# The next chunk's preparation moved from VectorE to TensorE, ScalarE and GpSimd, and D*u summed in y's bank

## The reference, cut to what matters

```python
up = y @ W_up + b_up                       # y: the normalised rows, normalised again, gamma, beta
left, right = split(up)                    # 128 channels each
u = silu(causal_conv3(left) + conv_b)
delta = softplus(u @ W_delta + b_delta);  Bm = u @ W_B;  Cm = u @ W_C     # 64 states
h = exp(delta * A) * h + (delta * u) * Bm  # token after token, 128 channels x 64 states
y = sum over states of h * Cm  + u * D
s = xn + (y * silu(right)) @ W_down + b_down
g = silu(sum of two experts of (silu(xn @ w1) * (xn @ w3)) @ w2)
out = x + s * g
```

## Time and profile before

| | |
|---|---|
| median of 3 runs | 1525.58 us (1524.34 to 1527.27) |
| profiled execution: its time, its span | 1526.07 us, 1524.3 us |
| busy: TensorE, VectorE, GpSimd, ScalarE | 80%, 80%, 76%, 47% of the span |
| first scan, and the chunks after the first begin | 103.5; 272.6, 437.0, 606.3, 778.3, 941.9, 1109.3, 1282.5 us |

### The profile page before, as it was taken

The page is one execution under the profiler, slowest core; times in us unless marked ns, Lnnn a source line. Parts: engine busy times, 40 slices in busy tenths (PEclk is TensorE's granted clock), DMA queues, the critical chain, the costliest instruction groups (busy, mean ns, idle before and its releaser), DMA issues. The chain is left out here.

```text
span 1524.3 us, 21337 instructions
## 1 busy us (share of the span) xinstructions
PE 1222.2 (80%) x5496; PEld 860.7 (56%) x5496; DVE 1222.3 (80%) x1597; ACT 721.6 (47%) x1557; POOL 1154.3 (76%) x1088
## 2 busy tenths in 40 slices
PE   5737655889988999889989999889988999896720
PEld 5613111566756677556666677657756676674410
DVE  6545999888787978799888987898778988787738
ACT  1445533464544555354555555455535555455611
POOL 0233788779896888778987888789977788799953
PEclk9969655899999999999999999999999999997555
DMA  9843697556564557446655855646744684754336
GB/s 239 168 128 94 169 283 206 150 151 189 172 224 132 171 165 254 129 133 204 220 158 160 250 171 158 228 126 208 232 140 127 181 259 149 255 166 145 121 117 221
DMA packets 173124, 272.52 MB, mean 179 GB/s; under 512 B 28544, under 2 KB 70144, under 8 KB 172992
## 3 DMA queue, kind: packets, MB, share of 16 engines
q10 hardware_dynamic: 111072, 173.93, 39.3%
q1 hardware_dynamic: 55104, 78.41, 16.7%
q0 software_dynamic: 6816, 18.69, 3.2%
HBM read 225.20 MB, written 45.76 MB: 178 GB/s over the span
## 5 line engine op out<-in xcount | busy, mean ns | idle before, releaser
L420 POOL TENSOR_TENSOR arena<-arena,c_rep 128x512 f32<-128x512 f32 x498 | 595.5, 1202 | 183.9 <-DVE arena L924 177.8
L924 DVE TENSOR_TENSOR_SCAN arena<-bank,carry,arena 128x512 f32<-128x512 f32 x512 | 651.9, 1274 | 75.2 <-ACT bank L660 69.9
L1154 PE MATMUL bank<-xgT,wring 128*128 128x256 f32 x2240 | 534.1, 381 | 17.8 <-DVE xn L952 7.1
L660 ACT ACTIVATE bank<-arena,a_neg 128x512 f32<-128x512 f32 x512 | 354.7, 693 | 261.5 <-DVE arena L924 111.0
L1154 PEld LDWEIGHTS bank<-xgT,wring 128*128 128x128 f32 x2240 | 424.0, 190 | 87.7 <-DVE gt L936 13.8
L1123 PE MATMUL bank<-wring,hid 128*128 128x256 f32 x1120 | 301.3, 392 | 44.9 <-ACT o_sb L604 44.6
L914 DVE TENSOR_TENSOR arena<-bank,b_rep 128x512 f32<-128x512 f32 x400 | 272.3, 681 | 40.4 <-PE bank L1166 32.4
L1166 PE MATMUL bank<-stack,pick 128*128 128x512 f32 x400 | 234.7, 598 | 73.3 <-DVE arena L914 51.9
L595 ACT ACTIVATE th<-bank 128x256 f32<-128x256 f32 x312 | 118.9, 381 | 367.6 <-PE bank L1154 309.2
L1123 PEld LDWEIGHTS bank<-wring,hid 128*128 128x128 f32 x1120 | 205.8, 192 | 150.2 <-issue 101.9
L442 POOL TENSOR_TENSOR hid<-gt,ue 128x256 f32<-128x256 f32 x312 | 244.9, 786 | 38.3 <-DVE gt L936 34.9
(11 more groups left out here) (148 smaller groups left out, 744.9 us busy)
## 6 DMA issues: line engine op xcount, KB each, us to landing
arena<-delta_d ACTq DMA_DIRECT2D x512, 256.0 KB, 4.0
arena<-du_d ACTq DMA_DIRECT2D x112, 256.0 KB, 4.2
wring<-in_w_all SPq DMA_DIRECT2D x64, 384.0 KB, 5.5
x_sorted<-arena SPq DMA_DIRECT2D x2, 5031.0 KB, 38.5
xg<-x_sorted ACTq DMA_DIRECT2D x39, 256.0 KB
arena<-results SPq DMA_DIRECT2D x16, 512.0 KB, 6.3
xn<-in_x SPq DMA_DIRECT2D x4, 1024.0 KB, 9.5
parts_d<-spare SPq DMA_DIRECT2D x16, 256.0 KB, 4.2
```

Source lines behind the costliest of these rows:

```text
L420: pool.tensor_tensor(p_ring[:, s % P_RING, :], h_ring[:, s % H_RING, :], of_chunk(c_rep, c, 2), ALU.mult).then_inc(s_hc, 1)
L660: act.activation(a_bank[s % 2][:, :], dl_ring[:, s % D_RING, :], ACT.Exp, scale=a_neg[:, s % PAIRS:s % PAIRS + 1]).then_inc(s_exp, 1)
L924: v.tensor_tensor_scan(out=h_ring[:, s % H_RING, :], data0=a_bank[s % 2][:, :], data1=product_with_b(s), initial=carry[:, q:q + 1], op0=AL ...
L1154: ins = pe.matmul(bank[:, m * SLOT:(m + 1) * SLOT], wring[:, kk, (2 * m + h) * P:(2 * m + h + 1) * P], xgT[:, i % 2, h, :], start=(h == 0) ...
```

## The change

VectorE's fourteen preparation instructions for a chunk and the final add of `gate_chunk` go.

- The convolution becomes three matmuls with diagonal weights (`taps`), a turn of its own at `at` 14; ScalarE evicts it.
- "1 + tanh", the clip, and the "1 + e, less 1" of the log's correction become ScalarE instructions, and so does the rounding of the high part. ScalarE has seven instructions more for a chunk.
- The products and sums of two tensors become seven GpSimd instructions for a chunk: `silu` and `right` at 17 and 18, `sum` in four parts at 25 to 28, `low` at 31.
- D*u is one more matmul with a diagonal weight, the first of a chunk into `y_bank`. SyncE's two stores and the load of `tails` go.
- The turns `delta`, `b` and `c` stand at 20, 23 and 26.

```diff
-WORK_AT = dict(conv=11, tanh=15, silu=16, clip=19, log=20, split=23, store=32, stack=36)
-WORK_PARTS = dict(conv=3, silu=3, log=2, split=7)
-PRODUCT_AT = {18: "delta", 21: "b", 24: "c"}
+WORK_AT = dict(tanh=15, sigmoid=16, silu=17, right=18, exp=22, ln=23, less=24, sum=25, round=30, low=31, store=33, stack=37)
+WORK_PARTS = dict(sum=4)
+PRODUCT_AT = {14: "conv", 20: "delta", 23: "b", 26: "c"}
 DOWN_AT = {6: 0, 8: 1}
-BIAS_AT, TAILS_AT = 61, 16
+BIAS_AT = 61
...
-            return spare[:, dict(cv=0, dlt=0, thl=1, ud=1, thr=2, sr=2, u=3, hi=3, ex=4, ln=5, lo=5, wm=6, du=6)[name], :]
+            return spare[:, dict(thl=0, hi=0, thr=1, du=1, u=2, cv=3, ex=3, ln=4, lo=4, dlt=5, wm=6)[name], :]
...
-        KD = 7
-        STORES = 16 * 6
+        KD, KS_P = 5, 6
+        STORES = 16 * 4
...
-                sp.dma_start(tails_d[:, 0, cols(c)], stage("sr")).then_inc(s_partd, 16)
-                sp.dma_start(tails_d[:, 1, cols(c)], stage("ud")).then_inc(s_partd, 16)
...
-                if at == TAILS_AT:
-                    sp.wait_ge(s_lr, NC)
-                    ge(sp, s_dn, 2 * c)
-                    sp.dma_start(tails[:, :, :], tails_d[:, :, cols(c)]).then_inc(s_tails, 16)
...
+            def silu_of_left(c):
+                pool.wait_ge(s_sig, c + 1)
+                if c:
+                    pool.wait_ge(s_red, QUADS * (c - 1) + 1)
+                pool.tensor_tensor(stage("u"), stage("thl"), stage("cv"), ALU.mult).then_inc(s_u, 1)
+            def gate_of_right(c):
+                pool.wait_ge(s_sig, c + 1)
+                ge(pool, s_dn, 2 * (c - 1))
+                pool.tensor_tensor(sr[:, c % 2, :], stage("thr"), b_rep[:, cols(c)], ALU.mult).then_inc(s_sr, 1)
+            def delta_sum(c, part):
+                base = KD * c
+                if part == 0:
+                    pool.wait_ge(s_sp, KS_P * c + 5)
+                    pool.tensor_tensor(stage("dlt"), stage("dlt"), stage("ln"), ALU.add).then_inc(s_dlt, 1)
+                elif part == 1:
+                    pool.wait_ge(s_sp, KS_P * c + 6)
+                    pool.tensor_tensor(stage("wm"), stage("wm"), stage("ex"), ALU.subtract).then_inc(s_dlt, 1)
+                elif part == 2:
+                    pool.wait_ge(s_dlt, base + 2)
+                    pool.tensor_tensor(stage("dlt"), stage("dlt"), stage("wm"), ALU.subtract).then_inc(s_dlt, 1)
+                else:
+                    pool.wait_ge(s_dlt, base + 3)
+                    pool.wait_ge(s_u, c + 1)
+                    pool.tensor_tensor(stage("du"), stage("dlt"), stage("u"), ALU.mult).then_inc(s_dlt, 1)
+            def low_part(c):
+                pool.wait_ge(s_hi, c + 1)
+                pool.tensor_tensor(stage("lo").bitcast(F32R), stage("du"), stage("hi"), ALU.subtract).then_inc(s_dlt, 1)
+            silu_of_left(0)
+            gate_of_right(0)
+            for part in range(4):
+                delta_sum(0, part)
...
+                for name, c, r in work_at(s):
+                    if name == "silu":
+                        silu_of_left(c)
+                    elif name == "right":
+                        gate_of_right(c)
+                    elif name == "sum":
+                        delta_sum(c, r)
+                    elif name == "low":
+                        low_part(c)
...
+            def evict_conv(c):
+                act.wait_ge(s_cv, c + 1)
+                ge(act, s_partd, STORES * c)
+                act.activation(stage("cv"), product_bank(c, "conv")[:, :], ACT.Identity, bias=half[:, 3:4]).then_inc(s_cvs, 1)
             def tanhs(c):
-                act.wait_ge(s_cv, c + 1)
+                act.wait_ge(s_cvs, c + 1)
                 act.activation(stage("thl"), stage("cv"), ACT.Tanh)
                 act.activation(stage("thr"), b_rep[:, cols(c)], ACT.Tanh).then_inc(s_tanh, 1)
+            def sigmoids(c):
+                act.wait_ge(s_tanh, c + 1)
+                act.activation(stage("thl"), stage("thl"), ACT.Identity, bias=1.0)
+                act.activation(stage("thr"), stage("thr"), ACT.Identity, bias=1.0).then_inc(s_sig, 1)
             def softplus(c, part):
                 if part == 0:
                     act.wait_ge(s_dp, c + 1)
                     act.activation(stage("ex"), product_bank(c, "delta")[:, :], ACT.Abs, bias=vec[:, 10:11]).then_inc(s_sp, 1)
+                    act.activation(stage("dlt"), product_bank(c, "delta")[:, :], ACT.Relu, bias=vec[:, 10:11]).then_inc(s_sp, 1)
                 elif part == 1:
-                    act.wait_ge(s_sp, 3 * c + 1)
+                    act.wait_ge(s_sp, KS_P * c + 1)
                     act.activation(stage("ex"), stage("ex"), ACT.Exp, scale=-1.0).then_inc(s_sp, 1)
+                elif part == 2:
+                    act.wait_ge(s_sp, KS_P * c + 3)
+                    act.activation(stage("wm"), stage("ex"), ACT.Identity, bias=1.0).then_inc(s_sp, 1)
+                    act.activation(stage("ln"), stage("ex"), ACT.Ln, bias=1.0).then_inc(s_sp, 1)
                 else:
-                    act.wait_ge(s_sp, 3 * c + 2)
-                    act.activation(stage("ln"), stage("ex"), ACT.Ln, bias=1.0).then_inc(s_sp, 1)
+                    act.wait_ge(s_sp, KS_P * c + 4)
+                    act.activation(stage("wm"), stage("wm"), ACT.Identity, bias=-1.0).then_inc(s_sp, 1)
+            def high_part(c):
+                act.wait_ge(s_dlt, KD * c + 4)
+                act.activation(stage("hi").bitcast(F32R), stage("du"), ACT.Copy).then_inc(s_hi, 1)
...
+            evict_conv(0)
             tanhs(0)
+            sigmoids(0)
...
-            for c in range(4, NC):
+            softplus(0, 3)
+            scale_rows(4)
+            scale_rows(5)
+            high_part(0)
+            for c in range(6, NC):
...
+            v.wait_ge(s_setup, 1)
+            for tap in range(3):
+                v.tensor_scalar(taps[:, tap, :], ident[:, :], half[:, tap:tap + 1], None, ALU.mult)
+            v.tensor_scalar(taps[:, 3, :], ident[:, :], vec[:, 11:12], None, ALU.mult)
...
-            def conv(c, tap):
-                cv = stage("cv")
-                if tap == 0:
-                    ge(v, s_partd, STORES * c)
-                    v.wait_ge(s_lrev, c + 1)
-                    v.tensor_scalar(cv, of_chunk(c_rep, c, 2), half[:, 2:3], half[:, 3:4], ALU.mult, ALU.add).then_inc(s_cvs, 1)
-                else:
-                    v.wait_ge(s_cvs, 2 * c + tap)
-                    v.scalar_tensor_tensor(out=cv, in0=of_chunk(c_rep, c, 2 - tap), scalar=half[:, 2 - tap:3 - tap],
-                                           in1=cv, op0=ALU.mult, op1=ALU.add).then_inc(s_cvs if tap == 1 else s_cv, 1)
...
-            def silu(c, part):
-                if part == 0:
-                    v.wait_ge(s_tanh, c + 1)
-                    v.scalar_tensor_tensor(out=stage("u"), in0=stage("thl"), scalar=1.0, in1=stage("cv"),
-                                           op0=ALU.add, op1=ALU.mult).then_inc(s_u, 1)
-                elif part == 1:
-                    v.scalar_tensor_tensor(out=stage("sr"), in0=stage("thr"), scalar=1.0, in1=b_rep[:, cols(c)],
-                                           op0=ALU.add, op1=ALU.mult).then_inc(s_ud, 1)
-                else:
-                    v.wait_ge(s_u, c + 1)
-                    v.wait_ge(s_ud, 2 * c + 1)
-                    v.scalar_tensor_tensor(out=stage("ud"), in0=stage("u"), scalar=vec[:, 11:12], in1=stage("sr"),
-                                           op0=ALU.mult, op1=ALU.mult).then_inc(s_ud, 1)
...
-            def clip(c):
-                v.wait_ge(s_sp, 3 * c + 1)
-                v.tensor_scalar(stage("dlt"), product_bank(c, "delta")[:, :], vec[:, 10:11], 0.0, ALU.add, ALU.max
-                                ).then_inc(s_dlt, 1)
...
-            def split(c, part):
-                dlt, du, wm = stage("dlt"), stage("du"), stage("wm")
-                hi, lo = (stage(name).bitcast(F32R) for name in ("hi", "lo"))
-                base = c * KD
-                if part == 0:
-                    v.wait_ge(s_sp, 3 * c + 3)
-                    v.tensor_scalar(wm, stage("ex"), 1.0, -1.0, ALU.add, ALU.add).then_inc(s_dlt, 1)
-                elif part == 1:
-                    v.wait_ge(s_dlt, base + 1)
-                    v.tensor_tensor(dlt, stage("ln"), dlt, ALU.add)
-                elif part == 2:
-                    v.wait_ge(s_dlt, base + 2)
-                    v.tensor_tensor(wm, wm, stage("ex"), ALU.subtract).then_inc(s_dlt, 1)
-                elif part == 3:
-                    v.wait_ge(s_dlt, base + 3)
-                    v.tensor_tensor(dlt, dlt, wm, ALU.subtract).then_inc(s_dlt, 1)
-                elif part == 4:
-                    v.wait_ge(s_dlt, base + 4)
-                    v.tensor_tensor(du, dlt, stage("u"), ALU.mult).then_inc(s_dlt, 1)
-                elif part == 5:
-                    v.wait_ge(s_dlt, base + 5)
-                    v.wait_ge(s_bc, 2 * c + 2)
-                    v.tensor_copy(hi, du).then_inc(s_dlt, 1)
```

(35 more changed lines are left out.)

42 lines of the change are left out of this document (20 added, 22 removed).

## The result

| | before | after |
|---|---|---|
| median (20 runs each) | 1527.03 us (1521.55 to 1530.24) | 1534.34 us (1528.03 to 1539.12) |
| ratio, 95% interval | | 1.0052 [1.0041, 1.0063] |
| profiled execution, its span | 1526.07, 1524.3 us | 1539.12, 1537.3 us |
| first scan | 103.5 us | 107.6 us |
| first chunk | 169.0 us | 173.7 us |

The changed kernel is 0.5% slower, where I forecast 0.7% faster. In the table, a chunk is taken from its first scan to the next chunk's. The parts of the table add up to the 13.0 us between the spans (4.1 + 4.7 + 6.0 - 1.8).

A forecast was written before the change was run, and what follows sets the result against it. TensorE was taken to set the pace at 32 to 63, GpSimd close behind, with VectorE the bound in the first chunk. 1526.1 - 9.6 (six chunks) - 4 (first chunk) + 3 (ahead of the loop) = 1515.5, forecast 1515; range 1495 to 1539.

The forecast's parts named there:

- SyncE's two stores and a load are off the path.: SyncE's queue: the two stores and the load were taken to cost the path nothing.
- (a): Chunk's end: VectorE's final add L945 goes, taking 10 us off TensorE's waits in six chunks; bounds 0 and 17.0.
- (b): Chunk boundaries: with about 2 us less to wait, TensorE's clock stays up, 12 us gained; bounds 0 and 14.
- (c): Gates, clip and B products behind VectorE's preparation: 13 of 16.8 us of TensorE's waits go; bounds 0 and 16.8.
- the convolution: TensorE at 8 to 15, 92% busy: three added products of 0.85 us a chunk hide nowhere, 15.3 us in six chunks.
- My sign: If right: TensorE's busy time at 8 to 15 rises about 2.5 us a chunk and the stretch is no shorter.
- GpSimd's lag: GpSimd, overfull at 24 to 31, falls one pair behind and catches up at 32 to 63: 5 us in six chunks.
- Two signs of "wrong": If wrong: waits for L476 or L411 to L426 over 10 us in all, or a clock below 1 at 24 to 40.
- GpSimd becomes the bound: Rival: preparation overloads GpSimd, hidden products come late, TensorE pauses and its clock drops: 1538 us; chance 0.24.
- The first chunk: First chunk, VectorE the bound: 4 us gained at 16 to 31, where GpSimd may lag; bounds 0 and -5.9.
- Ahead of the loop: Before the first scan: 13.4 us instead of 11.1 from u's first product to the first store; in all +3, bounds -1 and +7.

The follow-up runs named there:

- late_store: The changed kernel with SyncE's four stores at place 40 instead of 33 and the stack load at 48 instead of 37: 1517.89 us, ratio 0.9954.
- early_store: The kernel before with only SyncE's stores and stack load moved, to 27 and 31 instead of 32 and 36: 1558.24 us, ratio 1.0205.
- du_only: The kernel before with D*u alone as a matmul into y's bank, nothing else of the change: 1505.74 us, ratio 0.9874.
- ls_conv: late_store with the convolution back on VectorE at 11 to 13: 1506.46 us, ratio 0.9875.
- ls_both: late_store with the convolution and, in the loop, GpSimd's seven two-input instructions on VectorE: 1505.57 us, ratio 0.9873.
- ls_sums: late_store with GpSimd's seven two-input instructions on VectorE in the loop, at the same places: 1514.06 us, ratio 0.9927.
- mix_three: ls_conv with the second chunk's seven two-input instructions on VectorE; for other chunks, second and third sum and low part there, four on GpSimd: 1499.23 us, ratio 0.9812.
- late_all: The changed kernel with rounding at 34, low part at 36, SyncE's stores at 42 and stack load at 50: 1521.31 us, ratio 0.9982.

## Why the prediction was wrong

**"SyncE's two stores and a load are off the path."** This step failed. It was right for the stores that go, and I took it for the whole queue, so the sum put SyncE at nothing. That SyncE waits for GpSimd's low part, and that the tile's release stands behind it in the same list, was in the kernel (`store` at 33, `load_weights`), and nowhere in my sum. I had followed `high_part` into ScalarE's list, but not `low` into SyncE's. The runs show its price from both sides: 16 us taken away (late_store), 32 us put into the kernel before (early_store). With late_store's 1517.9 us, my 1515 would have been 3 us off, but partly by luck: against before, late_store's 8 to 31 are 7.6 us shorter, where my terms for them (-13, +15.3, +5) make 7.3 longer, and its first chunk is 4.6 us longer, where I had 4 shorter.

**(a) and (b), the boundary.** Right. Forecast -22, plus 5.1 for D*u's matmul (six of 0.85): -17. du_only's 0 to 7 shows -16.4, the changed kernel -14.2. The waits for the gate fell from 17.0 to 6.9 us, and du_only's boundary has the full clock; in the kernel after it is 1.00 in five of the six windows of 0 to 7 and 0.93 in one.

**(c), waits behind VectorE's preparation, and the convolution.** Forecast -13 and +15.3; measured together -9.8 at 8 to 23, and +1.6 at 24 to 31. The convolution alone costs 11.4 us (ls_conv against late_store), so the rest gave about 20, above the 16.8 that I had as (c)'s bound. Of these, du_only has 5.1 at 8 to 23 with the preparation still on VectorE; what of the others was paid back at 32 to 39 is not told apart. My sign, TensorE's busy time at 8 to 15 up by 2.5 us a chunk and the stretch no shorter, did not come: it fell from 141.2 to 138.5 us in all and the stretch by 5.8, with three steps moved out of it. The Trainium skill (SBUF — State Buffer, "Who interferes with whom") had me expect that the instructions moved to GpSimd would meet only VectorE instructions with one input in PSUM. They took 1.27 us instead of the 1.20 of `state_by_c`, and each of the 56 between 1.25 and 1.31, so none was held up. Where the rule does bite, it is as the two pairs of rows of ls_both above have it.

**GpSimd's lag, "5 us; bounds 0 and 15".** As a term it was not too small: in the profiled executions ls_sums has the six chunks 5.1 us and the first chunk 3.5 us shorter than late_store, and the medians differ by only 3.8 in all. What I didn't see is that it also decides when SyncE gets on. I had written that the rival needed a lag of more than two steps; in the timeline above `low` is 5.3 us behind its input, two pairs, and TensorE feels it through SyncE rather than through hidden products (5.5 us, three waits). Two signs of "wrong" came: the clock below 1 at 32 to 39, and ScalarE's waits for L421, 13.3 us over the span. The rival "GpSimd becomes the bound" gave 1538, near the 1534.3 measured, and named the clock's fall (its sum doesn't come out: 15 + 10 on 1515 make 1540, less the 5 already in it 1535); but GpSimd was no bound. It was busy 118.7 of 130.2 us (91%) at 24 to 31, where I had forecast over 95%, and moving SyncE's work alone won the time back.

As to the Trainium skill's rule that speaks against the change (GPSIMD Engine Reference, "Engine selection": two-input elementwise work belongs on VectorE, since GpSimd takes about twice as long): the rows above have 1.27 us on GpSimd against means of 0.72 to 1.50 on VectorE beside it, 1.08 over all seven, so not twice; twice holds against the 0.66 that VectorE takes undisturbed. My 1.84 and 1.90 for VectorE were the two slowest groups of the kernel before, which has 1.16, 1.12 and 1.01 for three of the others (L798, L792, L795). Its advice held where GpSimd was short of time, in the first chunk, and not in the others, where mix_three with four of the seven on GpSimd is the fastest.

**The first chunk, forecast -4, measured +4.7.** Wrong. I had GpSimd at 38.6 us for 16 to 31 and let it lag. The windows of the kernel after for 16 to 31 and 32 to 63:

```profile
170.10:210.50 40.40, 22.01 (x54) 6.42 (x54) 35.15 (x38) 19.11 (x32) 35.31 (x34) 0.61 0.58 147
210.50:281.30 70.80, 41.20 (x105) 12.94 (x106) 66.39 (x71) 23.62 (x41) 62.11 (x57) 0.50 0.85 251
```

One of VectorE's groups at 32 to 63, in the list of groups of that window:

```profile
L970 DVE TENSOR_TENSOR arena<-arena,c_rep 128x512 f32<-128x512 f32 x6 | 6.6, 1094 | 0.0
```

And two rows of the timeline:

```profile
207.13 0.63 ACT L611 ACTIVATE spare<-spare 128x512 fp32r<-128x512 f32 x1 [6.88 <-POOL spare L421]
...
208.48 1.28 DVE L936 TENSOR_TENSOR_SCAN arena<-bank,carry,arena 128x512 f32<-128x512 f32 x1 [3.58 <-ACT bank L733]
```

At 16 to 31 VectorE is idle 5.3 of 40.4 us instead of 1.2 of 39.6: ScalarE's rounding waited 6.88 us for GpSimd's last sum, and the scan 3.58 us for ScalarE behind it, the very order that I had described and put "inside the 5 us". Behind it, GpSimd works off what it owes, and L970, VectorE's own product with two inputs in SBUF, takes 1.09 us on average of six where it takes 0.68 in ls_both. Four took 0.68 here, two 1.68 and 2.17, as they met GpSimd's state by C: 2.5 of the 3.4 us lost there. With the sums on VectorE (ls_sums) the chunk takes 170.1 us, with the convolution there too (ls_both) 168.3.

**Ahead of the loop, forecast +3, measured +4.1.** Right. From u's first product to the first store the kernel after has

```profile
77.20 2.07 PE L1069 MATMUL bank<-spare,wdl 128*128 128x512 f32 x2 [4.49 <-POOL spare L398]
...
83.86 1.28 ACT L603 ACT_TABLE_LOAD   x1
...
85.86 1.27 POOL L411 TENSOR_TENSOR spare<-spare 128x512 f32<-128x512 f32 x1 [7.49 <-ACT spare L603]
...
93.07 0.33 SPq L305 DMA_DIRECT2D delta_d<-spare  x1
```

15.9 us instead of my 13.4: the table load is bare (1.28), and GpSimd's five are at 1.27. early_store, whose code ahead of the loop is that of before, had its first scan at 105.2 us against 103.5, so 1.7 us of such a difference can be chance.

**What stays open.** late_store, and all kernels with ScalarE's part and stores at 40 or later, keep 3 to 9 us more than before at 32 to 39 (114.6 to 120.2 against 111.4). GpSimd's lateness is 3.7 to 5.5 of them (mix_three and ls_both against ls_conv, ls_sums against late_store); for the last 3 or 4 no run here has the cause.

## What to carry to other kernels

- When a step moves to another engine, follow its result to every queue that waits for it, and list what stands behind that wait in the same queue. Here a bare semaphore increment for TensorE stood behind a store, and a preparation that was two or three pairs late cost 16 us through an engine that does no arithmetic at all. A wait at the head of an in-order queue is moved with two numbers.
- Test a change of several parts part by part. One matmul in place of one late VectorE add (and a product ahead of it) gave all of the gain at the boundary, 16.4 us, and 1.3% in all; the convolution on TensorE cost 11 us; the sums did best shared between two engines. That this is by where each had time is how I chose the shares, not something that a run singles out.
- A short wait of TensorE counts more than its length, when the clock falls behind it.

## What the runs showed of the hardware

- Behind waits of 4.8 and 5.6 us, eight 128x256 matmuls took 3.75 us, twice the usual 1.89: TensorE ran at 1.2 GHz. Behind waits of 1.5 us it kept 2.4 GHz, and behind one of 2.62 us eight took 1.97 us (late_all, 1222.39).
- A VectorE instruction with two inputs in SBUF and GpSimd's product of two SBUF tensors do not overlap freely. The one that began first kept its time in the rows of ls_both (0.66 us for VectorE's), and the other was longer by what it met (1.65 for VectorE's, 1.63 for GpSimd's). The seven groups' means on VectorE so spread from 0.72 to 1.50 us, with single instructions from 0.66 to 2.14.
- SyncE needed 2 us from the end of its last store's issue (542.91) to the release of TensorE's semaphore at 545.0. In it stand two register loads, of the tile's row and of its same-expert flag (L320 and L321, 0.66 and 0.58 us), which `load_weights` does ahead of its branch.
